# One tile for the transposed gated values and the transposed input, and one block scale, in an FP4 feed-forward stage

## The reference

```
numerator = einsum('bhld,bhmd->bhlm', q, k)
context = einsum('bhlm,bhmd->bhld', numerator / (sum(q) + EPS), v)
x = layernorm(x + context @ Wo + bo)
```

```
scale = max(max(abs(block)) / 6, 1e-12)
q = GRID[searchsorted(MID, abs(block / scale))] * sign(block) * scale
h = silu(q(x) @ q(w_gate).T) * (q(x) @ q(w_up).T)
x = layernorm(x + q(h) @ q(w_down).T)
```

## Time and profile before

| | |
|---|---|
| median of 3 runs | 815.86 us (815.85 to 816.23) |
| profiled execution | 815.38 us |
| its span, first to last instruction | 813.6 us |
| mean granted PE clock | 0.981 |
| busy: PE | 734.0 us, 90% |
| busy: DVE | 747.7 us, 92% |
| busy: ACT | 580.8 us, 71% |
| busy: POOL | 573.3 us, 70% |

### The profile page before, as it was taken

The page is one execution under the profiler, slowest core; times in us unless marked ns, Lnnn a source line. Parts: engine busy times, 40 slices in busy tenths (PEclk is TensorE's granted clock), DMA queues, the critical chain, the costliest instruction groups (busy, mean ns, idle before and its releaser), DMA issues.

```text
span 813.6 us, 20080 instructions
## 1 busy us (share of the span) xinstructions
PE 734.0 (90%) x4964; PEld 686.9 (84%) x4964; DVE 747.7 (92%) x1906; ACT 580.8 (71%) x1547; POOL 573.3 (70%) x613
## 2 busy tenths in 40 slices
PE   4999999999999968599899999999999999999994
PEld 3898888888888857599899899899899889889983
DVE  5999999999999998889999999999999999998883
ACT  3577777777777767477677777767767677768666
POOL 4676666666666655678778778778778878788762
PEclk9999999999999978899999999999999999999998
DMA  4122222212222110000000000000000000000002
GB/s 135 53 75 77 61 69 59 70 58 71 61 75 64 46 34 2 1 1 1 8 21 14 21 19 13 19 19 14 18 19 19 13 19 19 19 13 21 21 20 73
DMA packets 39718, 29.21 MB, mean 36 GB/s; under 512 B 3446, under 2 KB 39676, under 8 KB 39676
## 3 DMA queue, kind: packets, MB, share of 16 engines
q1 hardware_dynamic: 37228, 26.50, 10.6%
q10 hardware_dynamic: 2448, 2.23, 0.9%
HBM read 20.32 MB, written 8.39 MB: 35 GB/s over the span
## 4 chain that ended last, share of the span: by engine, by line
DVE 39%; PE 27%; issue 24%; DVEq 4%; POOL 3%; ACT 2%; DMA 0%; POOLq 0%; ACTq 0%; SPq 0%
PE bank L851 23%; DVE ln_t L624 3%; DVE ln_u L626 3%; DVE scratch L839 3%; DVE scratch L686 3%; DVE scratch L826 2%; DVE scratch L673 2%; DVEq L51 2%; DVE scratch L810 2%; DVE rounded L646 2%; DVE res L652 2%; PE wide L954 2%; DVE scratch L781 1%; DVE scratch L695 1%; DVE rstd L628 1%
## 5 line engine op out<-in xcount | busy, mean ns | idle before, releaser
L851 PE MATMUL bank<-wf_hi,rounded 128*128 128x352 f32 (+1 forms) x1792 | 409.8, 311 | 36.1 <-DVE rounded L832 21.6
L851 PEld LDWEIGHTS bank<-wf_hi,rounded 128*128 128x128 f32 x1792 | 301.8, 190 | 48.6 <-DVE rounded L832 28.3
L851 PE MATMUL bank<-wf_lo,rounded 128*128 128x352 f32 (+1 forms) x896 | 274.2, 306 | 0.0
L851 PEld LDWEIGHTS bank<-wf_lo,rounded 128*128 128x128 f32 x896 | 170.7, 191 | 0.0
L406 POOL TENSOR_TENSOR scratch<-scratch 128x704 f32<-128x704 f32 x64 | 95.8, 1497 | 97.8 <-DVE scratch L806 97.8
L851 PE MATMUL bank<-qkv_hi,rounded 128*128 128x512 f32 (+1 forms) x512 | 145.8, 339 | 0.0
L348 POOL TENSOR_TENSOR scratch<-scratch 128x512 f32<-128x512 f32 x64 | 67.9, 1061 | 75.8 <-DVE scratch L707 75.8
L390 POOL TENSOR_TENSOR scratch<-scratch 128x704 bf16<-128x704 f32 x64 | 100.4, 1569 | 1.8 <-ACT scratch L579 1.8
L851 PEld LDWEIGHTS bank<-qkv_hi,rounded 128*128 128x128 f32 x512 | 93.3, 191 | 9.9
L413 POOL TENSOR_TENSOR scratch<-scratch 128x704 f32<-128x704 bf16 x64 | 88.8, 1388 | 5.8 <-DVE scratch L810 0.7
L572 ACT ACTIVATE scratch<-scratch 128x704 uint8<-128x704 f32 x64 | 50.6, 791 | 52.8 <-POOL scratch L406 52.6
(11 more groups left out here) (102 smaller groups left out, 1771.6 us busy)
## 6 DMA issues: line engine op xcount, KB each, us to landing
scratch<-x_feat SPq DMA_DIRECT2D x64, 128.0 KB, 2.3
scratch<-x_tok SPq DMA_DIRECT2D x64, 128.0 KB, 2.0
out<-scratch SPq DMA_DIRECT2D x64, 128.0 KB, 1.7
scratch<-w_ffn ACTq DMA_DIRECT2D x17, 128.0 KB, 2.4
scratch<-L_attn_Wq SPq DMA_DIRECT2D x1, 256.0 KB, 2.7
scratch<-L_attn_Wk SPq DMA_DIRECT2D x1, 256.0 KB, 2.9
scratch<-L_attn_Wv SPq DMA_DIRECT2D x1, 256.0 KB, 3.7
wo<-L_attn_Wo SPq DMA_DIRECT2D x1, 256.0 KB, 3.2
```

The costliest lines, as they stand in the source:

```text
L851: last = pe.matmul(dst, x(c), w(c), start=first and n == 0, stop=n == len(terms) - 1)
```

## The change

The transposes of `hq` and of `xq` of one step go into one PSUM tile of eight chunks (`wide`, two banks): the input's two chunks first, the gated values' six behind. One semaphore `t_s` tells that both are done. One ACT copy makes the high parts of all eight chunks (`tr_hi`), one DVE subtraction the low parts (`tr_lo`), at the places where those of the gated values were (L554, L820). In the first and last steps, where only one of the two is live, the copy and the subtraction take that part alone (`turned`), and the first three still go through `pxt` (`tr_bank`). In the rounded scratch the eight chunks of the four buffers are interleaved, chunk by chunk. On the way back the scale is the slightly larger one whose reciprocal was taken (`bs2`; for the input and the weights `e_sc` and `w_sc` take the factor SHY = 1 + 2^-22), so POOL's scale `bsc` (L408) and its semaphore `h_sc` go, and DVE's `bs2` (L792) now awaits POOL's `hq` of two tiles before.

```diff
-        xqt_hi = [cube_r(KC, P) for _ in range(2)]
-        xqt_lo = [cube_r(KC, P) for _ in range(2)]
-        hqt_hi = [cube_r(IC, P) for _ in range(2)]
-        hqt_lo = [cube_r(IC, P) for _ in range(2)]
+        turned4 = cube_r(TC * 4, P).rearrange("p (c k) n -> p k c n", k=4)
+        tr_hi, tr_lo = ([turned4[:, 2 * j + k, :, :] for k in range(2)] for j in range(2))
...
+        def turned(i, t):
+
+            return slice(0 if live(i, t, 1) else KC, TC if live(i, t, -3) else KC)
+
+        def tr_bank(i, t):
+
+            if isinstance(i, int) and T * i + t < 3:
+                return pxt[:, 0:KC * P].rearrange("p (c n) -> p c n", c=KC)
+            return wide.rearrange("p (c n) -> p c n", c=TC)[:, turned(i, t), :]
...
-                        need(pool, x_t, m + 2 - T + 1)
+                        need(pool, t_s, m + 2 - T + 1)
...
-                        pool.tensor_scalar(bsc[b1], bmx[b1], 1.0 / 6.0, TINY, ALU.mult, ALU.max).then_inc(h_sc, 1)
                     if live(i, t, -2):
-                        need(pool, h_sc, m - 1)
-                        need(pool, h_t, m - 3)
+                        need(pool, t_s, m + 1)
                         need(pool, h_g, m - 1)
-                        pool.tensor_tensor(blocks(hq[b][:, 0:I]), blocks(hg[b]), over(bsc[b], NB),
+                        pool.tensor_tensor(blocks(hq[b][:, 0:I]), blocks(hg[b]), over(bs2[b], NB),
                                            ALU.mult).then_inc(h_q, 1)
...
-                    if live(i, t, -3):
-                        need(act, h_t, m - 2)
+                    if live(i, t, -3) or live(i, t, 1):
+                        need(act, t_s, m + 2)
+                        need(act, gu_b, m if live(i, t, 1) else NT)
                         need(act, d_s, m - 4)
-                        act.activation(hqt_hi[b1][:, :, :], wide[:, 0:IP].rearrange("p (c n) -> p c n", c=IC),
-                                       ACT.Copy).then_inc(h_hi, 1)
-                    if live(i, t, 1):
-                        need(act, x_t, m + 2)
-                        need(act, gu_b, m)
-                        act.activation(xqt_hi[b1][:, :, :], pxt[:, 0:KC * P].rearrange("p (c n) -> p c n", c=KC),
-                                       ACT.Copy).then_inc(x_hi, 1)
+                        act.activation(tr_hi[b1][:, turned(i, t), :], tr_bank(i, t), ACT.Copy).then_inc(t_hi, 1)
...
-                        need(dve, h_sc, m - 2)
...
+                        need(dve, h_q, m - 2)
                         dve.tensor_scalar(bs2[b1], bmx[b1], SHY / 6.0, TINY * SHY, ALU.mult, ALU.max).then_inc(h_s2, 1)
...
-                    if live(i, t, -3):
-                        need(dve, h_hi, m - 2)
+                    if live(i, t, -3) or live(i, t, 1):
+                        need(dve, t_hi, m + 2)
+                        need(dve, gu_b, m if live(i, t, 1) else NT)
                         need(dve, d_s, m - 4)
-                        dve.tensor_tensor(hqt_lo[b1][:, :, :], wide[:, 0:IP].rearrange("p (c n) -> p c n", c=IC),
-                                          hqt_hi[b1][:, :, :].bitcast(F32), ALU.subtract).then_inc(h_lo, 1)
+                        dve.tensor_tensor(tr_lo[b1][:, turned(i, t), :], tr_bank(i, t),
+                                          tr_hi[b1][:, turned(i, t), :].bitcast(F32), ALU.subtract).then_inc(t_lo, 1)
...
-                        need(dve, h_sc, m - 1)
...
-                    if live(i, t, 1):
-                        need(dve, x_hi, m + 2)
-                        need(dve, gu_b, m)
-                        dve.tensor_tensor(xqt_lo[b1][:, :, :], pxt[:, 0:KC * P].rearrange("p (c n) -> p c n", c=KC),
-                                          xqt_hi[b1][:, :, :].bitcast(F32), ALU.subtract).then_inc(x_lo, 1)
...
-                        need(pe, x_lo, m + 1)
+                        need(pe, t_lo, m + 1)
                         need(pe, h_a, m)
                         gate_up(0, b).then_inc(gu_a, 1)
-                    if live(i, t, -3):
-                        need(pe, h_q, m - 2)
-                        need(pe, h_lo, m - 3)
-                        for c in range(IC):
-                            last = pe.transpose(wide[:, c * P:(c + 1) * P], hq[b1][:, c * P:(c + 1) * P], ident[:, :])
-                        last.then_inc(h_t, 1)
-                    if live(i, t, 1):
-                        s = (t + 1) % T
-                        need(pe, x_q, m + 2)
-                        need(pe, x_lo, m + 1)
-                        for c in range(KC):
-                            last = pe.transpose(pxt[:, c * P:(c + 1) * P],
-                                                xq[:, s * D + c * P:s * D + (c + 1) * P], ident[:, :])
-                        last.then_inc(x_t, 1)
+                    if live(i, t, -3) or live(i, t, 1):
+                        need(pe, t_lo, m + 1)
+                        bank = tr_bank(i, t)
+                        at = turned(i, t).start
+                        if live(i, t, -3):
+                            need(pe, h_q, m - 2)
+                            for c in range(IC):
+                                last = pe.transpose(bank[:, KC + c - at, :], hq[b1][:, c * P:(c + 1) * P], ident[:, :])
+                        if live(i, t, 1):
+                            s = (t + 1) % T
+                            need(pe, x_q, m + 2)
+                            for c in range(KC):
+                                last = pe.transpose(bank[:, c - at, :],
+                                                    xq[:, s * D + c * P:s * D + (c + 1) * P], ident[:, :])
+                        last.then_inc(t_s, 1)
                     if live(i, t, -4):
-                        need(pe, h_lo, m - 3)
+                        need(pe, t_lo, m + 1)
                         need(pe, y_s, m - 4)
-                        three(pd[:, 0:D], lambda c: hqt_hi[b][:, c, :], lambda c: hqt_lo[b][:, c, :],
+                        three(pd[:, 0:D], lambda c: tr_hi[b][:, KC + c, :], lambda c: tr_lo[b][:, KC + c, :],
```

More of the change, by code:

```diff
@@ L65, in layer_kernel @@
     HALF = I // 2
+    TC = IC + KC
     NB = I // BLK
@@ L173, in layer_kernel @@
         hmg = [part(I // 2, BF16) for _ in range(2)]
-        bmx, bsc, bs2, binv = ([part(NB) for _ in range(2)] for _ in range(4))
+        bmx, bs2, binv = ([part(NB) for _ in range(2)] for _ in range(3))
         assert taken[0] <= until_post
@@ L206, in layer_kernel @@
             sem(f"e_{k}") for k in "max s2 inv sc xn y mg c g q".split())
-        x_t, x_hi, x_lo = sem("x_t"), sem("x_hi"), sem("x_lo")
-        gu_a, gu_b, si_a, si_b, h_a, h_b, h_max, h_s2, h_inv, h_sc, h_xn, h_y, h_mg, h_c, h_g, h_q = (
+        t_s, t_hi, t_lo = sem("t_s"), sem("t_hi"), sem("t_lo")
+        gu_a, gu_b, si_a, si_b, h_a, h_b, h_max, h_s2, h_inv, h_xn, h_y, h_mg, h_c, h_g, h_q = (
             sem(f"b_{k}") for k in
-            "gua gub sia sib ha hb hmax hs2 hinv hsc hxn hy hmg hc hg hq".split())
-        h_t, h_hi, h_lo, d_s, y_s, y_sm, y_nm, y_sq, y_ln, y_o = (
-            sem(f"b_{k}") for k in "ht hhi hlo d y ysm ynm ysq yln yo".split())
+            "gua gub sia sib ha hb hmax hs2 hinv hxn hy hmg hc hg hq".split())
+        d_s, y_s, y_sm, y_nm, y_sq, y_ln, y_o = (
+            sem(f"b_{k}") for k in "d y ysm ynm ysq yln yo".split())
         block = ctx.enter_context(nc.Block())
@@ L681, in attention @@
                         need(dve, w_qs, i)
-                        dve.tensor_scalar(w_sc, w_mx, 1.0 / 6.0, TINY, ALU.mult, ALU.max).then_inc(w_scs, 1)
+                        dve.tensor_scalar(w_sc, w_mx, 1.0 / (6.0 * SHY), TINY / SHY, ALU.mult, ALU.max).then_inc(w_scs, 1)
                     if live(i, t, -1):
@@ L800, in ffn @@
                         need(dve, x_q, 2 * (p - 1))
-                        dve.tensor_scalar(e_sc[e], e_mx[e], 1.0 / 6.0, TINY, ALU.mult, ALU.max).then_inc(e_scs, 1)
+                        dve.tensor_scalar(e_sc[e], e_mx[e], SHY / 6.0, TINY * SHY, ALU.mult, ALU.max).then_inc(e_scs, 1)
                     ln(2)
@@ L920, in gate_up @@
                     cols = slice(at + h * HALF, at + (h + 1) * HALF)
-                    last = three(dst[:, 0:HALF], lambda c: xqt_hi[b][:, c, :], lambda c: xqt_lo[b][:, c, :],
+                    last = three(dst[:, 0:HALF], lambda c: tr_hi[b][:, c, :], lambda c: tr_lo[b][:, c, :],
                                  lambda c: wf_hi[:, c, cols], lambda c: wf_lo[:, c, cols], KC)
```

## The result

The changed kernel takes 826.92 us (median of 4, 826.62 to 828.41) against 816.05 us before: a ratio of 1.0134, with a 95% interval of 1.0117 to 1.0152. It is slower by 10.9 us, as forecast in direction; 823 was forecast, with 829 as the upper end. The profiled execution is the slowest of the four, 828.41 us, with a span of 826.3 us.

The account below looks back on a forecast made before the run. The prediction took a loop of DVE through t = 1 to 3 and PE through t = 0 as the bound. Losses of 0.20 + 0.35 = 0.55 us over 13 passes gave 7.2 us, so 823 us; range 815 to 829.

Parts of the forecast that it names:

- What bounds the kernel: Feed-forward loop: DVE through t = 1, 2, 3 to the last subtraction, PE through t = 0, the Silu, DVE again; 29.93 us.
- its second term: At t = 0, PE's down product waits for DVE's late residual sum: 0.35 us more lost a pass.
- POOL's scale: Without it, one small norm instruction each at t = 2 and t = 3 waits for POOL's product, ending 0.85 us later.
- The subtraction: At t = 3, one merged subtraction lets PE restart 1.28 us after its start instead of 1.87: 0.59 less.
- The neighbours at the end of t = 2: Two successive norm instructions on DVE each wait for one POOL instruction; the second wait adds 0.62 us.
- the gain ahead of L614: At t = 2, POOL's addition starts 0.5 us earlier, so the norm's first DVE instruction ends 0.5 us earlier.
- the 0.5 is used up: By the end of t = 2 the earlier gain is spent, so DVE's product of t = 3 begins where it did before.
- The "bounds" sentence: Upward: t = 2's 0.5 us gain may be lost, t = 3 begins 0.47 later, a pass costs 1.02: 829 us.
- The residual sum at t = 0: DVE's residual sum comes 0.83 us later, and PE's down product waiting for it loses 0.35 us a pass.
- The merged copy: One ACT copy of 1.03 us for two; late only at t = 1, by 0.1 to 0.2 us, at no cost.
- the faster one: POOL between L406 and L413: equally slow without the scale, so 0.85 is never paid, 0.59 gained a pass: 808 us; chance 0.16.
- The case of no change: The 0.20 and 0.35 are cancelled by 0.4 at L624 and slack ahead of the down product: 816 us; chance 0.09.

Follow-up runs that it names:

- The run with ln(4) moved: Changed kernel with the layer-norm instruction ln(4) moved from in front of the merged subtraction to directly behind it: 826.64 us.
- the scale alone: Kernel before with only POOL's block scale removed, the gated values' product taking bs2; tiles, copies and subtractions stay two and two: 837.08 us.
- the tile alone: Changed kernel with POOL's block scale put back, so that only the tile is merged: 824.76 us.
- the fastest kernel: Changed kernel with the norm's intermediate products in PSUM, and the norm's first two instructions and the input pair's scale moved later on DVE: 789.68 us.

## Why the prediction was right, and where it was off

**What bounds the kernel**: right. DVE through t = 1 to 3, PE through t = 0; DVE idle once a pass, at t = 1 (1.36 us). The run with ln(4) moved shows that the loop closes through the residual sum as much as through the subtraction, which the forecast had as its second term.

**POOL's scale**: right in place and size. L628 and L630 went from 0.15 to 1.00 and 0.99 us, and the scale alone costs 21 us. What the forecast said of the lock itself, two inputs in SBUF, is too narrow: L612, one of its own examples, is a `tensor_scalar` with one.

**The subtraction**: 1.28 forecast from start to PE's restart, 1.26 measured (524.30 to 525.56).

**The neighbours at the end of t = 2**: right. 517.76 and 518.32 wait for one POOL instruction each.

**The term that was mis-sized** is the gain ahead of L614, taken as 0.5 us: measured from t = 1's L767 it ends at 8.56 (511.42 - 502.86) and before at 8.82 (508.28 - 499.46), 0.26. The reason is in the rows at 504.65 and 504.14: L794 (`bs2`) takes 0.60 us instead of 0.17, since POOL's L408, itself stretched to 1.08 us behind DVE's L789, is in front of it. It is not the new wait for `hq`: the tile alone has no such wait, and `bs2` takes 0.61 us there. POOL comes to t = 1 0.4 us later than before: t = 0's reciprocal starts 4.10 us ahead of the next L767 (529.48 to 533.58) instead of 4.50 (524.89 to 529.39), as DVE is late behind L624, and L399 then waits for ACT's mask, which it did not before. In the walk the prediction let the norm's last instruction of t = 2 end 0.09 earlier than before (515.1 against 515.19); measured from L767 of t = 1 it ends 0.27 later (16.00 against 15.73). Of these 0.36 between walk and trace, 0.24 is the missing gain and 0.12 is L399, which starts 1.82 after L415's end instead of 1.7. So L767 of t = 3 starts at 15.92 (518.78) after t = 1's, not at 15.66 (515.12, by the same view of the kernel before): 0.26 late, where "the 0.5 is used up" had it unmoved. With it PE starts t = 0 0.42 later (22.70 against 22.28), not 0.20. The "bounds" sentence had this very loss, up to 0.47.

**The residual sum at t = 0**: forecast 0.35, measured 0.25: the down product starts 3.07 us after the step (525.56 to 528.63) instead of 2.82. Another 0.12 is lost before the next L767 (4.95 from the down product's start instead of 4.83). Sum 0.42 + 0.25 + 0.12 = 0.79 measured against 0.55 forecast. The forecast that PE's wait for the residual sum would rise from 2.4 us to 5 to 7 failed: it is 2.6, since the wait at t = 2 that made up the old 2.4 (0.18 in the row at 508.75) is gone and one of 0.24 at t = 0 has come in its place.

**The merged copy**: in the loop it costs nothing, as forecast (at the end of the kernel it does, see the total). At t = 1, where it might have been late, L823 starts 0.42 us after the product ahead of it (506.02 to 506.44), as it would without any wait.

**The total**: the two profiled spans differ by 12.7 us (the medians by 10.9). Twelve passes, 380 to 749 us, lost 9.3 of that, the next one 0.4 and the time before them 0.25, where the forecast had 13 x 0.55 = 7.2. The end of the kernel, behind the last t = 1, lost 2.75 (47.7 us for 44.95), and for that the forecast had nothing: it counted fewer waits on semaphores, and passed over one that is new. In the last pass, where only the gated values are still live, the merged copy awaits the last `gate_up(1)` (`need(act, gu_b, m if live(i, t, 1) else NT)`), which stands behind the down product in PE's list; the copy before had no such wait:

```profile
798.67 0.81 ACT L562 ACTIVATE rounded<-wide 128x768 fp32r<-128x768 f32 x1 [4.31 <-PE bank L848]
...
799.51 0.96 DVE L823 TENSOR_TENSOR rounded<-wide,rounded 128x768 fp32r<-128x768 f32 x1 [1.90 <-ACT rounded L562]
...
800.52 0.87 PE L954 MATMUL wide<-ident,scratch 128*128 128x128 f32 x6 [1.94 <-DVE rounded L823]
802.76 0.55 PE L848 MATMUL bank<-wf_hi,rounded 128*128 128x256 f32 x1 [1.36 <-DVE res L771]
```

PE's two stands (1.94 and 1.36 us) are followed by a granted clock of 0.50 from 802 to 808 us, with 0.55 us for the first product there; in the kernel before PE also stands (2.15 us ahead of 794.55) and its clock stays at 1.00 to the last product. The wait of 4.3 us is in all eight runs with the merged tile and in none without. A run that drops it was not made. So the upper bound of 829 held without a term for this, and its margin was narrower than it looks.

**The rivals**: the faster one rested on POOL being slow between L406 and L413; L420 starts 0.04 before L415's end (514.91 and 514.87). The rule of the Trainium skill on the number of instructions (VectorE: DVE Perf Modes, Rules for kernel authors) named there does not decide here: 60 Vector instructions fewer went with 11 us more. The case of no change needed L624 (now L626) to get past POOL's next instruction; it took 0.54 us behind it.

## What to carry to other kernels

When DVE has small instructions with two SBUF operands (here also a `tensor_scalar` with one) beside a busy GpSimd, read their durations one by one: a 128x4 product that takes 1.4 us is waiting, and its price is set by where it falls in the other list, not by its size. Any edit to either list, a removal too, shifts these meetings, so look first whether they can be taken away (an operand in PSUM, a place where GpSimd is idle) and judge the edit only then: the scale's removal changed the time by +21 us on the kernel before, +2 with the merged tile, -15 with the norm's products in PSUM and -17 with the norm in POOL's idle stretch. The merged tile changed it by +9 us on the kernel before, -10 with the scale gone and +4 with the norm in POOL's idle stretch. And read the waits of the unrolled ends apart from those of the loop.

## What was not expected of the hardware

Moving two intermediate tiles of 4 columns to PSUM took 27 us off an 827 us kernel, and the instruction is no slower for it: 0.15 us, as in SBUF with POOL idle. The wait does not depend on how little DVE wants: 128x4 numbers wait up to 1.35 us, until the end of a GpSimd instruction on 128x704. Two neighbours can each wait for a fresh GpSimd instruction (0.52 and 0.54 us at 517.76 and 518.32 in the changed kernel, where the second needs the first's result). That is not confined to dependent ones, as DVE's order of time in the fastest kernel shows, at t = 2 and at t = 0 of one pass (L784 is the input pair's scale here, L795 that of the gated values):

```profile
525.80 0.57 DVE L616 TENSOR_SCALAR ln_v<-row_sq 128x4 f32 x1
526.28 0.17 DVE L784 TENSOR_SCALAR scratch<-scratch 128x32 f32<-128x32 f32 x1
...
540.31 0.75 DVE L784 TENSOR_SCALAR scratch<-scratch 128x32 f32<-128x32 f32 x1
540.98 0.67 DVE L795 TENSOR_SCALAR scratch<-scratch 128x44 f32<-128x44 f32 x1
```

L784 follows L616 at once, though POOL's L409 starts at 526.31. But L784 and L795, which don't need each other either, end with POOL's L400 (541.03) and its L409 (541.61). What decides who goes next is not shown.
